# A graph-network kernel: count and weight matrices built beside the first dense product instead of behind it

## The reference

```
L0: x1 = h @ W1 + b1                          # 1024 -> 512
    g = x1; 4 times: g = g + sum over edges of norm * tanh(g[dst].a + g[src].b + c) * g[src]
    f = concat(x1, g)
L1: W = zeros(1024, 1024).at[src, dst].add(edge_weight);  f = h @ W.T + bias
L2: f = relu(normalised sum over edges and self loops of (h @ W2)[src] + b2)
L3: attention over edges: weights exp(-leaky_relu(al[src] + ar[dst])), summed by src, then elu
```

## Time and profile before

| | |
|---|---|
| median of 3 runs (lowest to highest) | 1062.14 us (1062.12 to 1064.44) |
| the profiled execution, and its span | 1068.09 us, 1066.6 us |
| TensorE busy | 997.6 us (94%), x5168 |
| VectorE busy | 694.1 us (65%) |
| ScalarE busy | 426.3 us (40%) |
| GpSimd busy | 156.6 us (15%) |
| mean granted TensorE clock | 0.971 of 2.4 GHz |
| ACT_TABLE_LOAD on ScalarE (L1040), one | 1.28 us |
| GpSimd's adds L848 under the dense product, mean of nine | 1.29 us |
| `w_lo` (L459) in the first product, eight | 4.89 us |

### The profile page before, as it was taken

How to read it: one execution, slowest core, us unless ns; L and a number is a source line. 1 busy time by engine, 2 the same in 40 slices (tenths; PEclk the granted TensorE clock), 3 DMA queues, 4 the chain that set the end, 5 groups by cost and what they waited for, 6 DMA issues and landing times.

```text
span 1066.6 us, 15082 instructions
## 1 busy us (share of the span) xinstructions
PE 997.6 (94%) x5168; PEld 826.5 (77%) x5168; DVE 694.1 (65%) x1380; ACT 426.3 (40%) x693; POOL 156.6 (15%) x203
## 2 busy tenths in 40 slices
PE   5798858999999999998999999999999999999997
PEld 4576746888888887777888888878887888788876
DVE  6675988778877797834347434314464664888886
ACT  4132877454555365511224333224222222354443
POOL 2223120000000002143222100001100000233331
PEclk9798987999999999998999999999999999999999
DMA  5232335000000001254442212042443121102223
GB/s 186 93 133 95 130 155 205 14 1 21 0 0 20 0 0 60 88 193 189 179 148 106 99 45 74 1 158 98 138 159 98 65 100 58 40 1 79 79 79 113
DMA packets 27361, 93.28 MB, mean 87 GB/s; under 512 B 3274, under 2 KB 3742, under 8 KB 27316
## 3 DMA queue, kind: packets, MB, share of 16 engines
q1 hardware_dynamic: 16116, 52.82, 14.1%
q0 software_dynamic: 11200, 39.86, 10.1%
HBM read 64.35 MB, written 28.32 MB: 87 GB/s over the span
## 4 chain that ended last, share of the span: by engine, by line
PE 81%; DVE 8%; ACT 4%; issue 3%; DMA 3%; POOL 1%; ACTq 0%; DVEq 0%; POOLq 0%
PE ps L538 31%; PE ps L1907 12%; PE ps L1825 8%; PE ps L1826 8%; PE ps L1827 8%; PE ps L1879 4%; PE ps L1880 4%; PE ps L521 3%; DMA x_after<-xres 2%; PE ps L1805 1%; DVE stats L467 1%; DVE hT_lo L511 1%; DVE mask L1425 1%; ACT count_row L1003 1%; ACT hT_hi L504 1%
## 5 line engine op out<-in xcount | busy, mean ns | idle before, releaser
L538 PE MATMUL ps<-w_hi,hT_hi 128*128 128x512 f32 x400 | 162.9, 407 | 14.5 <-DVE hT_lo L511 10.4
L1825 PE MATMUL ps<-g_hi,mask_hi 128*128 128x512 f32 x400 | 160.0, 400 | 7.8 <-DVE mask_lo L1430 7.8
L538 PE MATMUL ps<-w_lo,hT_hi 128*128 128x512 f32 x400 | 159.3, 398 | 0.0
L1826 PE MATMUL ps<-g_lo,mask_hi 128*128 128x512 f32 x400 | 157.6, 394 | 0.0
L1827 PE MATMUL ps<-g_hi,mask_lo 128*128 128x512 f32 x400 | 157.3, 393 | 0.0
L538 PE MATMUL ps<-w_hi,hT_lo 128*128 128x512 f32 x400 | 133.0, 398 | 0.0
L511 DVE TENSOR_TENSOR hT_lo<-ps,hT_hi 128x1024 fp32r<-128x1024 f32 x40 | 49.0, 1224 | 99.7 <-ACT hT_hi L504 99.7
L1907 PE MATMUL ps<-y_all,att_hi 128*128 128x512 f32 x400 | 109.8, 392 | 2.5 <-ACT gat_sums L1175 1.3
L1055 ACT ACTIVATE mask<-ps,v 128x640 f32<-128x640 f32 x80 | 63.4, 794 | 116.6 <-PE ps L1827 55.6
L538 PEld LDWEIGHTS ps<-w_hi,hT_hi 128*128 128x128 f32 x400 | 77.1, 193 | 32.5 <-DVE hT_lo L511 14.3
L1825 PEld LDWEIGHTS ps<-g_hi,mask_hi 128*128 128x128 f32 x400 | 76.2, 190 | 27.7 <-DVE mask_lo L1430 6.3
(11 more groups left out here) (181 smaller groups left out, 1788.4 us busy)
## 6 DMA issues: line engine op xcount, KB each, us to landing
xin<-x_after SPq DMA_DIRECT2D x30, 512.0 KB, 3.3
xres<-x_after POOLq DMA_DIRECT2D x20, 512.0 KB, 4.0
x_after<-xres POOLq DMA_DIRECT2D x20, 512.0 KB, 3.2
w_raw<-in_L_gnn_W SPq DMA_DIRECT2D x8, 1024.0 KB, 6.9
x_after<-xres POOLq DMA_DIRECT2D x20, 256.0 KB, 3.1
xres<-x_after SPq DMA_DIRECT2D x10, 512.0 KB, 3.4
xin<-in_x SPq DMA_DIRECT2D x9, 512.0 KB, 4.0
xres<-in_x POOLq DMA_DIRECT2D x18, 256.0 KB, 4.8
```

Of the source, the lines that this page charges most:

```text
L538: last = nc.tensor.matmul(PRODUCT[d.n][b][:, half * BANK:(half + 1) * BANK], left[:, k, :], right[:, k, half * BANK:(half + 1) * BANK], st ...
L1825: nc.tensor.matmul(SUMS[dd], mask_hi[k][:, cols], g_hi[:, s, :], start=(s == 0), stop=False)
L1826: nc.tensor.matmul(SUMS[dd], mask_hi[k][:, cols], g_lo[:, s, :], start=False, stop=False)
```

## The change

The building no longer follows the first dense product but is cut in 25 groups and laid into it. A tile's product has four places, in front of every second k; from tile 2 on each place holds one group (`groups_at`: VectorE makes cells two groups ahead), the weight rows of a finished node tile one place later and its count rows two places later (`tiles_behind`). The product keeps one bank for each of two tiles (`PRODUCT0`), the count sums have one pair of banks instead of two, and the rows share another. ScalarE evicts a group's counts and weights with one instruction each, and evicts x1; the bias comes in as a 25th matmul of a tile, of 33 rows (ones against the bias's high part in row 0 and its rest in row 32). Edge rows have 125 edges, without padding. The picking matmuls stand ahead of tile 0's product; ScalarE copies what they picked. Three of the eight `w1_lo` go to GpSimd. Completeness is judged early, by counting unused slots (`captured`, `judge`). GpSimd's adds for the first 512 columns now run behind the stores of the rows, in one loop with those of the second 512 (m from 0 to 19). Seven (before: five, behind the building) of the ten gate dot products lie under the last tiles. Operands at 128 partitions of edges become 125.

```diff
-ROW_EDGES = 128
-EDGE_ROWS = -(-E // ROW_EDGES)
-EDGE_TILES = -(-EDGE_ROWS // P)
-NO_NODE = 2000
+EP = 125
+EDGE_TILES = 2
+EDGE_ROWS = E // EP // EDGE_TILES
+SPARE = WINDOWS * EP - E
 RING = 3
 HALF_GROUP = PER_GROUP // 2
-ROWS_BEHIND = 2
-QW = 4
+FIRST_STEP = 2
+PER_STEP = 4
+LEAD = 2
+BIAS_ROWS = 33
+POOL_LOW = (2, 5, 7)
...
+    CELL_SUMS = ps[:, 0:2 * BANK].rearrange("p (n c) -> p n c", c=BANK)
+    ROWS = ps[:, 2 * BANK:4 * BANK]
+    COUNT_ROWS = ps[:, 2 * BANK:2 * BANK + NP // 2].bitcast(BF16)
...
+    def groups_at(t, place, lead):
+
+        g = PER_STEP * (t - FIRST_STEP) + place + lead
+        return [g] if 0 <= g < CELL_GROUPS else []
+
+    def tiles_behind(t, place, behind):
+
+        g = PER_STEP * (t - FIRST_STEP) + place - behind
+        return [a for a in range(T) if last_group(a) == g]
...
+        load_edges(dst_rows, dst, dst_landed)
         sp.dma_start(xin[1][:, :], x[P:2 * P, :]).then_inc(xin_landed[1], 16)
-
-        def load_edges(to, of, landed):
-
-            whole, rest = E // ROW_EDGES, E % ROW_EDGES
-            sp.dma_start(to[:, 0, :], of[0:P * ROW_EDGES].rearrange("(p c) -> p c", c=ROW_EDGES)).then_inc(landed, 16)
-            sp.dma_start(to[0:whole - P, 1, :], of[P * ROW_EDGES:whole * ROW_EDGES].rearrange("(p c) -> p c", c=ROW_EDGES)
-                         ).then_inc(landed, 16)
-            sp.dma_start(to[whole - P:whole - P + 1, 1, 0:rest], of[whole * ROW_EDGES:E].rearrange("(p c) -> p c", c=rest)
-                         ).then_inc(landed, 16)
-
-        sp.wait_ge(pads_done, 3)
-        load_edges(dst_rows, dst, dst_landed)
         load_edges(src_rows, src, src_landed)
         load_edges(ew_rows, edge_weight, ew_landed)
-        load_weights(sp, d, w1)
-        sp.dma_start(b1_all[:, :], b1.partition_broadcast(P)).then_inc(consts_landed, 16)
+        for q in range(4):
+            sp.dma_start(w1_raw[:, 2 * q:2 * q + 2, :], w1[2 * q * P:(2 * q + 2) * P, :].rearrange("(k p) n -> p k n", p=P)
+                         ).then_inc(w_landed[q], 16)
+        sp.wait_ge(consts_done, 5)
...
+        for t in range(2, T):
+            n = min(P, N - t * P)
+            sp.wait_ge(h_transposed[t % 2], t // 2)
+            sp.dma_start(xin[t % 2][0:n, :], x[t * P:t * P + n, :]).then_inc(xin_landed[t % 2], 16)
...
+        for k in POOL_LOW:
+            pool.wait_ge(w_hi_ready, k + 1)
+            nc.gpsimd.tensor_tensor(w1_lo[:, k, :], w1_raw[:, k, :], w1_hi[:, k, :].bitcast(F32),
+                                    ALU.subtract).then_inc(w1_lo_pool, 1)
+        pool.wait_ge(bias_hi_ready, 2)
+        pool.wait_ge(w1_lo_pool, len(POOL_LOW))
+        low_row = slice(BIAS_ROWS - 1, BIAS_ROWS)
+        nc.gpsimd.tensor_tensor(bias_r[low_row, :], b1_raw[low_row, :], bias_r[low_row, :].bitcast(F32),
+                                ALU.subtract).then_inc(bias_ready, 1)
...
+        for m in range(2 * T):
+            t = m % T
+            pool.wait_ge(half_landed[m % 4], 16 * (m // 4 + 1))
+            if m < T:
+                pool.wait_ge(product_read[t % 2], t // 2 + 1)
+            else:
+                pool.wait_ge(sum_read, T * (GATES - 1) + t + 1)
+            nc.gpsimd.tensor_tensor(half[m % 4], half[m % 4], g[:, t, :], ALU.add).then_inc(half_added, 1)
+            pool.wait_ge(half_added, m + 1)
+            pool.dma_start(x1_dram[t * P:(t + 1) * P, m // T * HID:(m // T + 1) * HID], half[m % 4]).then_inc(half_stored[m % 2], 16)
+            if m >= 1:
+                pool.wait_ge(half_stored[(m - 1) % 2], 16 * ((m - 1) // 2 + 1))
+                if m + 3 < 2 * T:
+                    load_half(m + 3)
 
 
...
+            moved(countT, windows, 0, T).then_inc(counts_copied, 1)
...
+        def take_x1(t):
+
+            act.wait_ge(product_ready[t % 2], t // 2 + 1)
+            nc.scalar.activation(g[:, t, :], PRODUCT0[t % 2], ACT.Copy).then_inc(product_read[t % 2], 1)
+
+        def place_act(t, place):
+
+            for n in groups_at(t, place, 0):
+                take_cells(n)
+            for a in tiles_behind(t, place, 1):
+                if a < WT_TILES:
+                    take_weight_rows(a)
+            for a in tiles_behind(t, place, 2):
+                take_count_rows(a)
+
...
+        act.wait_ge(bias_landed, 32)
+        nc.scalar.activation(bias_r[0:BIAS_ROWS, :], b1_raw[0:BIAS_ROWS, :], ACT.Copy).then_inc(bias_hi_ready, 1)
+        act.wait_ge(ends_picked, 2)
+        for n in range(2):
+            nc.scalar.activation(edges[0:EP, n, :], PICKED[n][0:EP, 1, :], ACT.Copy).then_inc(picked_copied, 1)
+        act.wait_ge(parts_picked, 3)
+        for n in range(2, 5):
+            nc.scalar.activation(edges[0:EP, n, :], PICKED[n][0:EP, 1, :], ACT.Copy).then_inc(picked_copied, 1)
+        for t in range(T):
+            if t + 1 < T:
+                transposed_act(act, d, (t + 1) // 2, (t + 1) % 2)
+            place_act(t, 0)
+            if t > 0:
+                take_x1(t - 1)
+            place_act(t, 1)
+            if t + 2 < T:
+                root_act(act, d, (t + 2) // 2, t % 2)
+                h_act(act, d, (t + 2) // 2, t % 2)
+            if t == FIRST_STEP:
+                act.wait_ge(complete_ready, 1)
+                whole = act.value_load(complete[0:1, 0:1], min_val=0, max_val=1)
+            place_act(t, 2)
+            place_act(t, 3)
...
+        for n in range(2):
+            act.wait_ge(product_read[n], 1)
+            g_split(n)
         tanh(0, 0, 0, 0)
-        g_split(0)
+        act.wait_ge(count_stored[0], 16 * HT)
+        tanh(0, 0, 0, 1)
         mask_hi_of(0, 0)
-        g_split(1)
-        for s in range(1, TANH_LEAD):
-            tanh(0, 0, 0, s)
+        take_x1(T - 1)
+        tanh(0, 0, 0, 2)
...
+        def place_dve(t, place):
+
+            for n in groups_at(t, place, LEAD):
+                cells(n)
+            for a in tiles_behind(t, place, 1):
+                count_rows_of(a)
 
...
+        stats_dve(dve, d0, 0, 0)
+        scale_dve(dve, d0, 0, 0)
+        rows_before()
+        stats_dve(dve, d0, 0, 1)
+        scale_dve(dve, d0, 0, 1)
+        pick_rows()
+        transposed_dve(dve, d0, 0, 0)
+        for k in range(KT):
+            if k not in POOL_LOW:
+                dve.wait_ge(w_hi_ready, k + 1)
+                nc.vector.tensor_tensor(w1_lo[:, k, :], w1_raw[:, k, :], w1_hi[:, k, :].bitcast(F32),
+                                        ALU.subtract).then_inc(w_lo_ready, 1)
+        for t in range(T):
+            if t != FIRST_STEP:
+                place_dve(t, 0)
+            if t == T - 2:
+                gates(2, 2)
+            if t != FIRST_STEP:
+                place_dve(t, 1)
+            if t == T - 2:
+                gates(3, 3)
+            if t + 2 < T:
+                stats_dve(dve, d0, (t + 2) // 2, t % 2)
+            if t == 0:
+                blend_ends()
+            if t + 1 < T:
+                transposed_dve(dve, d0, (t + 1) // 2, (t + 1) % 2)
+            if t + 2 < T:
+                scale_dve(dve, d0, (t + 2) // 2, t % 2)
+            if t == 0:
+                name_cells()
+                blend_parts()
+            if t == 1:
+                judge()
+            if t == FIRST_STEP:
+                dve.wait_ge(complete_ready, 1)
+                whole = dve.value_load(complete[0:1, 0:1], min_val=0, max_val=1)
+            if t == T - 2:
+                gates(4, 4)
+            if t == FIRST_STEP:
+                place_dve(t, 0)
+                place_dve(t, 1)
+            place_dve(t, 2)
+            place_dve(t, 3)
+            if t == T - 3:
+                dve.wait_ge(gw_landed, 16)
+                dve.wait_ge(consts_landed, 16)
+                nc.vector.tensor_copy(gb_col[:, :], gb[:, 0:1]).then_inc(gb_chain, 1)
+                dve.wait_ge(gb_chain, 1)
+                gates(0, 0)
+                gates(1, 1)
+            if t == T - 1:
+                gates(5, 5)
+                gates(6, 6)
...
+            pe.wait_ge(counts_copied, g)
+            pe.wait_ge(weights_taken, min(g, WEIGHT_GROUPS))
...
+        def x1_pe(t):
+
+            b = t % 2
+            pe.wait_ge(hT_lo_ready, t + 1)
+            pe.wait_ge(product_read[b], t // 2)
+            if t == 1:
+                pe.wait_ge(blend_chain, 3)
+            if t + 1 < T:
+                transpose_pe(pe, d0, (t + 1) // 2, (t + 1) % 2)
+            for k in range(KT):
+                if k % 2 == 0:
+                    place_pe(t, k // 2)
+                if t == 1 and k == KT // 2:
+                    sum_captured()
+                if t == T - 1 and k == KT // 2:
+                    pe.wait_ge(product_read[0], HT)
+                    spread_u(0, 0)
+                if t == 0:
+                    below = len([n for n in POOL_LOW if n < k])
+                    if k in POOL_LOW:
+                        pe.wait_ge(w1_lo_pool, below + 1)
+                    else:
+                        pe.wait_ge(w_lo_ready, k - below + 1)
```

(31 more changed lines are left out.)

492 lines of the change are left out of this document (202 added, 290 removed).

## The result

Median 1049.36 us (four runs, 1045.73 to 1053.56), against 1062.99 for the kernel before beside it (1062.12 to 1064.44): ratio 0.985, 95% interval 0.982 to 0.988. Run once more among the last experiments it had 1049.84 against 1067.53, ratio 0.982 (0.977 to 0.987). The medians lie 13.6 us apart beside each other here and 17.7 there (15.8 and 19.3 by the ratios), where 20 were forecast. The profiled execution went from 1068.1 to 1049.4.

A forecast was written before the change was run, and what follows sets the result against it. Dense product (bound by TensorE) and building (VectorE, then ScalarE) ran one behind the other. Gates 24.3 us earlier, less 3.9 in the first gate half and 0.4 at read-outs, gave 20 off the 1062.1 median: 1042, forecast 1036 to 1049, range 1030 to 1055.

The forecast's parts named there:

- Opening, 55.3: From the start through tile 2's step, with picking, first weights and first groups: ends at 55.3 us.
- Steps of tiles 3 to 6, 14.5 each: Interleaved product and building: TensorE's 13.3 us plus a wait of about 1.2 a step, 58 us for four.
- Tiles 7 and 8, 11 and 8.5: Last interleaved steps before tile 9: 11 us for tile 7 and 8.5 for tile 8.
- Gates at 142: First gate product, after tile 9's step: at 142 us with the adds, instead of 166.3, so 24.3 us gained.
- First gate half, 3.9 back: GpSimd's ten residual adds now run beside VectorE's masks there and cost 3.9 us of the gain.
- two adds lie in it: VectorE's work up to the second source tile's mask_lo: two adds of 1.2 lengthen 5.7 us to 8.1.
- The gain of 0.9: First gate half: the bound for no contention at all between adds and VectorE, a gain of 0.9 us.
- The low clock that goes gives nothing: Start of the first gate half: losing TensorE's low clock saves 0 us, since VectorE is late next.
- Read-outs, 0.4 back: Behind the gates, the residual loop's wait for each previous tile's store costs 0.4 us, bounds 0 and 4.
- Deeper overlap: Rival, chance 0.18: steps at TensorE's 13.3 us and adds falling between VectorE's operations, 11 us less, 1031.
- Half clock: Rival, chance 0.04: TensorE idle over some 2.4 us twice an interleaved step drops to low clock, 1092 us.
- Steps of 17: Rival, chance 0.15: interleaved steps take 17 us instead of 14.5, opening 3 later, 13 more, 1055.

The follow-up runs named there:

- e5: Changed kernel with ScalarE's order in a step made root, copies of the third place's group, then h, instead of copies behind h; 1041.87 us, ratio 0.977.
- e1: Changed kernel without GpSimd's adds of the first half of each residual row, but for two numbers a tile; 1041.84 us, ratio 0.980.
- e2: Changed kernel with GpSimd's first ten residual adds made to wait for mask_lo of later source tiles, everything computed; 1041.36 us, ratio 0.979.
- e7: On top of e2, three of the five adds at the last gate half's start wait until behind VectorE's wt_lo; 1036.96 us, ratio 0.970.
- e11: On top of e9, gate dot products of tiles 5 and 6 moved into the first gate half, adds one source tile later; 1030.29 us, ratio 0.964.
- e9: Changed kernel with the edits of e2, e5, e7 and e8 joined; 1028.29 us, ratio 0.962.
- e12: On top of e9, all eight w_lo of the first weights on VectorE, none on GpSimd; 1029.18 us, ratio 0.964.
- e8: Changed kernel with the residual loop waiting for the store of the tile before only where a load follows; 1047.69 us, ratio 0.983.
- the two edits behind the first half: Three of the last gate half's adds placed behind wt_lo (e7, 1036.96 us on top of e2); no store wait where no load follows (e8, 1047.69 us).
- e3: Changed kernel with ScalarE copying out the third place's group ahead of both root and h; 1052.82 us, ratio 0.989.
- e10: The changed kernel run once more, unaltered, beside the last experiments; 1049.84 us.

## Why the prediction was right, step by step

*Opening, 55.3.* 54.9 in the profile of the result, 51.1 to 53.7 in other profiles of the same opening. I took 5.1 us for VectorE's five `w_lo`, and they take 4.2 or 6.3; the low clock in tile 2's step takes up to 1.7 more or not. No single number could have been right, and that mine was within 0.4 is in part luck: TensorE's own register read, for which the sum has 1.7, doesn't show (the transposes of tile 3's step follow the product before them at 54.89 without a pause), and VectorE's costs 0.73 and not 1.7; the cells of group 2 came 0.8 later than I had them all the same.

*Steps of tiles 3 to 6, 14.5 each.* 14.25: 13.4 of work and 0.85 of wait on the mean, at the fourth place, released by ScalarE, where I had 13.3 and 1.2. The 1.2 was not worked out: 7.9 against 7.3 and more gives 0.6 at most. e5 shows that the place of h is the cause. The merged copies saved next to nothing (0.72 + 0.40 against 0.63 + 0.45), where I took 0.18 a group.

*Tiles 7 and 8, 11 and 8.5.* 11.7 and 8.8.

*Gates at 142.* 142.95, 139.6 when run again. e1 puts 2.5 us of it on two adds, where I had put 0.5; without them tile 9's part is shorter than I had it, by 0.6.

*First gate half, 3.9 back.* Right in its cause, too small in size: 5.6. The term that failed is "two adds lie in it" and one each in the third and fourth tiles. I counted four adds, 4.8 us, from tanh to the fourth source tile; six lie between 137.9 and 160.7, and e1 gives them 7.7 us, 2.5 ahead of the gate product and 5.2 behind it. The gain of 0.9 that I set against them isn't there either: without adds the stretch takes 27.8 us and not 26.4. But e1, e2, e7 and e11 have 3.4 us at the low clock in it; in e9 and e12, which have none, it takes 26.5. "The low clock that goes gives nothing" was right beside the adds (32.9 with 6.8 us of it, 32.7 without any), though it did not go in the first profile, and wrong without them: there the profiles with it are 1.3 us longer. The Trainium skill's rule (SBUF — State Buffer, Summary: rules for kernel authors), that such operations shut each other out wholly, is what the lengths show: 1.0 to 1.5 us more for each add of 1.28. That the later one waits is not what the starts show: in seven of the nine meetings VectorE's operation started first, by 0.04 to 0.33 us, and was drawn out, while the add kept its 1.27 to 1.31 (GpSimd's times in a profile are rough). I let a little under half of the ten reach TensorE, and it was six of ten, since the first tiles leave VectorE no room.

*Read-outs, 0.4 back.* 27.7 against 27.1 us up to the residual, and 0.6 by e8.

*Rivals.* Deeper overlap (1031) did not come by itself; with ScalarE's order and the adds' places mended, and the two edits behind the first half (some 4 us), the kernel runs at 1028. Half clock: 1.00 in all of the steps. But the 2.4 us from which I let it decide is no border: in e3's steps 2.34 was enough. Steps of 17: only in e3, from ScalarE's order.

The total: 24.3 - 3.9 - 0.4 = 20 had been forecast. Up to the residual 23.3 - 5.6 - 0.5 - 0.5 = 16.7 came out (the last but one term, from `spread_u` to the transposes, had none in the forecast), and the profiled executions lie 18.7 apart; what is between is scatter of the later stages, which take 580.7 to 587.0 us from the residual on in the fourteen profiles. The median, 1049.4, lies 7 us above my 1042 and at the upper edge of the narrower forecast, 1036 to 1049. Of the 7, 1.3 are the 18.7 us for 20. The other 6 come from taking the 20 off the median of the kernel before, though its profiled execution was 6 us longer: that of the changed kernel, forecast at 1048, took 1049.4, no longer than its own median. What made the one before longer stays open; the medians of the kernel before beside the experiments were 1063.8, 1066.5 and 1067.5.

## What to carry to other kernels

When work is moved beside a busy engine, ask of every two-input SBUF operation of GpSimd what VectorE is doing at that moment and whether anyone waits for VectorE: the same ten adds cost 7.7 us at the start of the gates and nothing four source tiles later. When three engines share a step, a single buffer between two of them is paid where the reader's queue has something long ahead of the read; move the short operation that releases the next engine to the front, then the read, then the long one. Price a moved group at both ends of its new place, not by a mean.

## What the hardware showed

VectorE's operation that reads PSUM beside SBUF is not held up: the five `g` updates take 3.47 us with an add of GpSimd beside them (e2, 387.61) and without (174.40). Custom dot products, which read SBUF twice, are: 0.75 to 1.96. The add can be the one that is drawn out, too: 1.72 us for 1.28 (e2, 153.04). The same code can settle into either of two patterns of collision (6.3 or 4.2 us). The length of TensorE's pause alone doesn't tell which clock follows: after 2.04 us (e1) and 2.59 the products came at the low clock; after 2.01 (e9), 1.65 and even 3.29 (e10) at the full one.
